# Cross-attention and an RWKV block on one core: another merge table for the nine streams of steps

## The reference

```python
# block 0: attention of the queries over context and queries, 16 heads of 16, then an MLP
q  = x @ q_w + q_b                                   # 256 queries
kv = concat([ctx, x]) @ kv_w + kv_b                  # 768 keys
attn = softmax(where(mask, q.k / 16, -inf))          # 16 heads, 256 x 768
y  = attn.v @ out_w + out_b + x
y  = gelu(rmsnorm(y) * w @ mlp_w1 + b1) @ mlp_w2 + b2 + x
# block 1: RWKV time mix, 32 heads of 8, then a channel mix
xa = layernorm(y);  sx = shift(xa) - xa
xxx = tanh((xa + sx * maa_x) @ maa_w1)               # five low-rank mixes k, w, v, r, g
xk, xw, xv, xr, xg = xa + sx * (maa_stack + xxx @ maa_w2)
w = exp(-exp(decay + tanh(xw @ td_w1) @ td_w2)); r, k, v, g = xr@Wr, xk@Wk, xv@Wv, silu(xg@Wg)
for t in range(256):                                 # per head, state S is 8 x 8
    out[t] = r[t] @ (u * k[t] v[t]' + S);  S = k[t] v[t]' + w[t] * S
y1 = y + groupnorm(out) * g @ Wo.T
xc = layernorm(y1);  xk, xr = mixes of xc and shift(xc)
return y1 + sigmoid(xr @ Wfr.T) * (relu(xk @ Wfk.T)**2 @ Wfv.T)
```

## Time and profile before

| what | value |
|---|---|
| median of 3 runs | 513.42 us (508.31 to 544.58) |
| the profiled execution's own time | 513.0 us |
| its span, first to last instruction | 511.2 us |
| PE busy, matmuls | 439.4 us (86%) x2676 |
| DVE busy | 326.7 us (64%) x623 |
| ACT busy | 215.3 us (42%) x417 |
| POOL busy | 105.3 us (21%) x103 |
| mean granted TensorE clock | 0.929 |

### The profile page before, as it was taken

How to read it: one execution, slowest core, us unless ns; L and a number is a source line. 1 busy time by engine, 2 the same in 40 slices (tenths; PEclk the granted TensorE clock), 3 DMA queues, 4 the chain that set the end, 5 groups by cost and what they waited for, 6 DMA issues and landing times.

```text
span 511.2 us, 7173 instructions
## 1 busy us (share of the span) xinstructions
PE 439.4 (86%) x2676; PEld 263.4 (52%) x2676; DVE 326.7 (64%) x623; ACT 215.3 (42%) x417; POOL 105.3 (21%) x103
## 2 busy tenths in 40 slices
PE   4988789899999999999899897999999896975465
PEld 2753323335774445577455355765462684662344
DVE  1245775733438578876897879688696646488342
ACT  1540523575636545643545455344558231400011
POOL 7350110010101004240100315220335101013000
PEclk9995955999999999999999999999999997996668
DMA  7799990350234274200237012001600000000001
GB/s 265 241 297 304 374 341 5 79 131 0 96 91 131 79 164 126 63 2 1 63 84 166 2 41 53 12 0 35 154 23 21 1 1 0 0 0 2 0 0 41
DMA packets 24137, 44.56 MB, mean 87 GB/s; under 512 B 2436, under 2 KB 18468, under 8 KB 22952
## 3 DMA queue, kind: packets, MB, share of 16 engines
q1 hardware_dynamic: 23112, 42.58, 28.3%
q10 hardware_dynamic: 992, 1.54, 0.9%
HBM read 29.53 MB, written 14.42 MB: 86 GB/s over the span
## 4 chain that ended last, share of the span: by engine, by line
PE 67%; DVE 21%; ACT 5%; issue 4%; DMA 1%; POOL 1%; SPq 0%; DVEq 0%; ACTq 0%; POOLq 0%
PE pW L432 10%; PE pO L490 8%; PE pMX L459 8%; DVE mx L979 8%; PE pST L473 7%; PE pW L515 6%; PE pW L577 5%; PE pW L586 5%; PE pW L528 4%; ACT probs L711 3%; DVE A L936 3%; PE pW L500 2%; PE pW L440 2%; PE pW L655 1%; DMA Wkq<-w_kq 1%
## 5 line engine op out<-in xcount | busy, mean ns | idle before, releaser
L979 DVE TENSOR_REDUCE mx<-pMX 128x1 f32<-128x512 f32 (+1 forms) x192 | 122.8, 685 | 46.2 <-PE pMX L459 44.8
L711 ACT ACTIVATE probs<-pST 128x512 f32<-128x512 f32 x192 | 104.2, 596 | 63.4 <-PE pST L473 62.0
L459 PE MATMUL pMX<-Kst,Qst 97*128 97x512 bf16 (+1 forms) x256 | 72.1, 358 | 14.3 <-DVE mx L979 13.8
L473 PE MATMUL pST<-Qst,Kst 99*128 99x256 bf16 x384 | 65.2, 282 | 1.8 <-ACT probs L711 0.2
L490 PE MATMUL pO<-probs,Vn 128*32 128x256 f32 x768 | 63.5, 403 | 0.3 <-ACT probs L711 0.3
L473 PEld LDWEIGHTS pST<-Qst,Kst 99*128 99x128 bf16 x384 | 30.3, 99 | 42.1 <-ACT probs L711 23.6
L459 PEld LDWEIGHTS pMX<-Kst,Qst 97*128 97x128 bf16 x256 | 20.7, 100 | 58.7 <-DVE mx L979 45.1
L936 DVE TENSOR_TENSOR_SCAN A<-four,COL,A 128x256 f32<-128x256 f32 x64 | 48.9, 825 | 0.3
L515 PE MATMUL pW<-hT,Wkq 128*128 128x256 f32 (+1 forms) x96 | 34.1, 507 | 7.3 <-DMA Wkq<-w_kq 7.3
L1111 DVE SCALAR_TENSOR_TENSOR A<-pW,COL,A 128x256 f32<-128x256 f32 (+1 forms) x24 | 13.0, 570 | 27.3 <-ACT A L757 18.5
L843 POOL TENSOR_TENSOR A<-A 128x1024 bf16<-128x1024 f32 x8 | 17.0, 2128 | 60.7 <-ACT A L725 60.7
(11 more groups left out here) (139 smaller groups left out, 601.2 us busy)
## 6 DMA issues: line engine op xcount, KB each, us to landing
Kst<-k_stack SPq DMA_DIRECT2D x16, 576.0 KB
A<-v_rows SPq DMA_DIRECT2D x6, 1024.0 KB, 9.6
k_stack<-A SPq DMA_DIRECT2D x8, 576.0 KB, 4.3
k_stack<-A SPq DMA_DIRECT2D x8, 384.0 KB, 2.9
Qst<-q_stack SPq DMA_DIRECT2D x16, 192.0 KB
hT<-hT SPq DMA_DIRECT2D x3, 768.0 KB, 4.8
q_stack<-A SPq DMA_DIRECT2D x16, 128.0 KB, 3.3
Wsq<-w_sq SPq DMA_DIRECT2D x1, 2048.0 KB, 14.4
```

The lines of the kernel that those rows point to most:

```text
L459: last = mm(pMX[n % 2][:, at:at + hi - lo], Qst[s][0:R_MASK + 1, h, qt * P:(qt + 1) * P], Kst[s][0:R_MASK + 1, h, lo:hi], start=True, stop ...
L473: last = mm(pST[n % ST_BANKS][:, i, :], Kst[s][0:R_LO + 1, h, nt * P:(nt + 1) * P], Qst[s][0:R_LO + 1, h, :], start=True, stop=True)
L711: act_fn(probs[n % UNITS_P][:], pST[n % ST_BANKS][:], ACT.Exp, scale=1.0 / DH)\
L979: v.tensor_reduce(dst, src, AX.X, ALU.max).then_inc(max_done, 1)
```

## The change

The table ORDER is replaced by another one. Streams, steps, instructions, waits, buffers and banks stay; what differs is where the steps of one stream stand among those of the others, and so the order in which each engine meets them. The diff, cut to the first and the last line of the table:

```diff
-ORDER = ("k5 v2 k v3 0 s2 k v k5 v m15 k m s2 k m2 x k2 m k m2 x3 m x s m16 x k x m4 x m4 x2 m5 x5 m3 x m2 x m4 x m2 "
...
-         "33 23 33 26 38 23 33 25 32 2 39 2 39 2 328 22 38 ")
+ORDER = ("k6 v4 s k2 s k3 m5 k m2 0 m8 s2 m8 s x m2 v m3 v m2 x2 m2 x m x m x m4 k2 x4 m3 x m x2 m2 x2 m2 x2 m5 x4 m3 "
...
+         "25 x6 3 x19 23 33 23 33 24 3 22 38 2 35 2 35 22 3 2 326 22 35 2 3 23 35 2 33 2 37 ")
```

## The result

| | changed kernel | kernel before |
|---|---|---|
| median of 22 runs each | 505.8 us | 510.6 us |
| ratio, with 95% interval | 0.992 (0.9895 to 0.9943) | 1 |
| profiled execution, its span | 503.3 us, 501.5 us | 513.0 us, 511.2 us |
| mean granted clock in it | 0.942 | 0.929 |

The changed kernel is 0.8% faster. So what a stretch is worth has to be read from several traces; the experiments give them. The comparisons leave out runs over 1.5% above the fastest of a kernel, so a ratio and a median of all runs can differ.

The account below looks back on a forecast made before the run. PE was taken as the bound nearly everywhere, so only its lost time could be won. From the profiled 513.0 us, 7 less to group 4, 1 less in the middle and 0 in the last batch gave 505 us; range 497 to 519.

Parts of the forecast that it names:

- Term 1: The start, to the first exp: fill 0 at 31.2 us, 3.6 us earlier, and first exp at 47.2 instead of 51.3.
- Term 2: Groups 0 to 3, first exp to first exp of group 4: ends at 109.4 instead of 116.6, 7 us less.
- no gain at the start: Rival, chance 0.25: the run of 22 fills lets the clock fall early, so the extra work costs double; 512 us.
- SP's loads: Stack 3 and group 1's 2 KB load, queued behind weights on SP: costed at nothing.
- Term 3: The middle, from the first exp of group 4: 1 us less, bounds 6 less and 13 more.
- Unit m behind its last fill: Item in the middle: unit m no longer directly follows its last fill; 1.7 us less.
- Slow rival: Chance 0.17: POOL's kv1 stops DVE on the fills' path, three times 4.52 us; 520 us.
- L1092: Sign in the new profile: this small DVE instruction, which had ended with POOL's kv1, never takes over 0.3 us.
- Term 4: The last batch, from the last exp on, with xcT, kk, xr and rr of batch 2 moved: 0, bounds 3 either way.
- -1.7 for wo and ogT at the high clock: Item in the last batch: kk and rr keep PE busy, so wo takes 2.0 instead of 3.78, ogT 0.4 instead of 1.1.
- xr on the path: Item in the last batch: xr right ahead of groot is wholly on the path, 1.0 us more.

Follow-up runs that it names:

- Experiments five: New order to unit m of group 0, with batch 1's three V units put later, then the old order; against the kernel before: ratio 1.002.
- six: Old order to unit m of group 0, new order to the first exp of group 4, then old; against the kernel before: ratio 0.987.
- experiment ten: Kernel before with fills 24 to 47 spread evenly between unit m of group 1 and the first exp of group 1: 512.8 us, ratio 1.008.
- experiment twelve: Kernel before with fills 38 to 47 moved behind group 1's first exp, spread evenly with the next stretch's fills; run of twelve kept: 501.7 us, ratio 0.984.
- experiment eight: Kernel with new start, old middle, new end; unit m of group 13 and two fills moved behind the next pv and exp: 0.993 of before.
- experiment nine: Changed kernel with kv0 of batch 1 and its followers moved behind fills 160 to 162, away from POOL's kv1: 1.007 of the kernel before.
- experiment three: Old order to oq of the last group, new order behind it; against the kernel before: 508.8 us, ratio 0.995.
- experiment seven: Kernel with new start, old middle, new end; batch 2's xr moved behind gout and rr behind wo of batch 3: 505.6 us, 0.988 of before.

## Why the prediction was right, and where its steps were not

505 us stood against a median of 505.8 and a profiled 503.3, and the range held both. Part of that is luck. The 505 were counted from 513.0, and before's median of 22 runs is 510.6: as a difference I forecast 8 us, 1.6%, and the medians show 4.8, the ratio 0.8%. And two errors partly cancel: the middle's sign and the end's gain.

- **Term 1, fill 0 at 31.2, first exp at 47.2.** 31.1 and 47.1, with 2.58 us of idle PE ahead of fill 0 where I had 1.6; the load was issued at 24.65 (I had 24.2). In the other traces of this start fill 0 came at 31.5 to 32.7. The 4.2 us of lead were paid back, as my sum had it, by the three V units that term 2 takes in (3 x 1.73 = 5.2 us). Experiments five and six show the balance as nothing.
- **Term 2, first exp of group 4 at 109.4.** 106.3 in the profile, 107.3 to 108.2 in the other traces with this start. Work and loss were both sized too high: I had 55.0 + 7.2 us. In the profile PE is busy 55.3 of 59.2 us at clock 0.97, so by the same working as in the term the work at full clock is 53.6 us and the loss 5.6. "So PE, no longer DVE, sets the pace there" is right for the new order, where PE is busy 20.0 of 20.8 us and DVE's share of group 0's stretch is 64%, 76% before. In the old one DVE was not the only bound, since PE at half clock was busy 90% of the low part. But the reason beside it, "no run of fills there is longer than five, where the old one had twelve in a row", is wrong (experiment ten). I counted "three fills less in the stretch" up to group 4 and did not cut it at group 1, where 31 fills became 17. That is the step that was missing, and by experiment twelve it carries the gain.
- **Rival "no gain at the start".** It decides at a clock below 0.85 from the first exp to group 4; the rows of group 0 and of groups 1 to 3 give (20.8 x 0.91 + 38.4) / 59.2 = 0.97. A part of its mechanism was there: by the granted clock the low level began at 33.8 us, behind the idle time ahead of fill 0, and not at 39.6 as before.
- **SP's loads** cost nothing, as I had it: from 44 to 112 us the changed kernel's PE waits for fills, oTs and four, and for no load.
- **Term 3, the middle, 1 us less.** It is 3 us more by the traces and about 4 by the ratios, inside the bounds of 6 less and 13 more, on their other side. I counted the waits of the old order that went and left new ones out, such as the one ahead of fill 116 for DVE. The low clocks, most of the 3 us, were in no item. Unit m behind its last fill, as an item, also fell short: such an idle time of 2.1 us grew to 5.0 when the unit was moved behind the next pv and exp (experiment eight).
- **Slow rival, POOL stops DVE.** In the changed kernel kv0 stretches to 4.77 us and PE does not feel it, for the reason I gave (exps behind it need no DVE). In experiment nine 3.8 us of the same kind stood in front of a fill, with DVE 2.8 us late already, and together they cost about 8. L1092 stayed at or below 0.37 us, just over my 0.3. So 0.17 was not too much for this rival.
- **Term 4, the last batch, 0.** 1.7 us less by the mean of the traces, 2.5 by the ratio of experiment three. -1.7 for wo and ogT at the high clock was the right item (1.99 us instead of 3.78; experiment seven shows that it takes rr in the hole too: with kk alone there wo took 3.78). xr on the path cost 0.6, not 1.0, and the new order won some 1.2 us ahead of maa1 of batch 3, not 0.6 (last oq to maa1: 32.9 to 33.3 us in seven traces of the old order there, 31.7 to 32.2 in seven of the new).

Summed: start -7 (ratio 0.987), middle +4, end -2.5 by the runs, against my -7, -1 and 0. The start came out at my number, but by experiment twelve what carries it is the count of fills ahead of group 1, which I had not looked at.

## What to carry to other kernels

Where one engine's work feeds another in order, count both engines' work between two fixed steps of the list: a stretch with 31 reductions (24.8 us of DVE work) for 18.5 us of matmuls was slow however it was mixed, and ten of them moved one stretch later were worth at least as much as the whole new start, and twice the whole new table (1.6% against 0.8%). An earlier start of a stretch that then runs on another bound was worth nothing here, and a step moved in a shared list moves on every engine's queue: look up what it passes on each. With one profile of each kernel a stretch is known to some 3 us only; halves of the change in traces of their own told more than the pair did.

## What the runs showed of the hardware that was not expected

- The granted clock differs between executions of the same kernel. In one session of 21 runs of before they went from 505.1 us at a mean clock of 0.948 to 517.6 us at 0.920, and one run of the changed kernel took 637 us at 0.64. The old middle had no, one or two low spots of 3.4 us, in different places, in ten traces of ten kernels that share it.
- An idle PE was paid twice: beside 5.05 us of waiting stood 10.3 us at 1.2 GHz, beside 4.96 us 6.8, and with 2.56 us of waiting ahead of ogT the low clock went on for another 5.6 us, where with 0.78 it had ended.
- DVE was slowed by short POOL instructions as well as by the long one: four scans took 4.63 us instead of 2.67 beside two of 1.5 us.
